# Moving the issue of a transposed activation's stores from one DMA queue to another in a fused attention and FFN kernel

## The reference

```python
x = x + xattn(layernorm(x), ctx, ctx, Wt, Wp, Wg, Wz, gn_w, gn_b)
x = x + ffn(layernorm(x), up, down, perm)

# xattn, per sample: t = Wt @ ctx, p = Wp @ layernorm(x), g = Wg @ ctx
att = sum over each of the 8 channel groups of (p * g)      # one number per group
y = Wz (block diagonal, 8 blocks of 64) @ (att * t)
out = groupnorm(y) * gn_w + gn_b + ctx

# ffn, per row of 2048: 16 heads of 128 columns picked by perm
t = gelu(t[:, perm] as (16, 128) @ up[h]) @ down[h], columns put back by the inverse of perm
```

## Time and profile before

| | before |
|---|---|
| median of three runs | 1584.0 us |
| lowest and highest | 1579.34 and 1595.7 us |
| the profiled execution | 1595.7 us, span 1593.9 us |
| mean granted TensorE clock | 0.986 |
| TensorE, VectorE, ScalarE, GpSimd busy | 95%, 75%, 67%, 61% of the span |

### The profile page before, as it was taken

How to read it: one execution, slowest core, us unless ns; L and a number is a source line. 1 busy time by engine, 2 the same in 40 slices (tenths; PEclk the granted TensorE clock), 3 DMA queues, 4 the chain that set the end, 5 groups by cost and what they waited for, 6 DMA issues and landing times.

```text
span 1593.9 us, 19526 instructions
## 1 busy us (share of the span) xinstructions
PE 1519.4 (95%) x6592; PEld 1240.8 (78%) x6592; DVE 1196.9 (75%) x1480; ACT 1066.9 (67%) x1317; POOL 977.2 (61%) x781
## 2 busy tenths in 40 slices
PE   8998879996999999999999999999999999998998
PEld 6876667875888878888788887888788887876776
DVE  5777767874788767886678876787778877878776
ACT  4634727671787738866488845878468773897876
POOL 1695646257792538917386255853579354887886
PEclk9999989998999999999999999999999999999999
DMA  8798867878476855779467783668837676759786
GB/s 319 267 317 338 247 198 276 290 219 258 138 270 240 252 163 169 265 252 260 130 195 274 255 251 122 218 251 251 251 121 264 248 233 191 252 152 258 257 280 215
DMA packets 176467, 374.79 MB, mean 235 GB/s; under 512 B 24561, under 2 KB 90097, under 8 KB 168177
## 3 DMA queue, kind: packets, MB, share of 16 engines
q1 hardware_dynamic: 151024, 281.25, 55.8%
q0 software_dynamic: 25344, 92.29, 16.5%
HBM read 287.45 MB, written 86.03 MB: 234 GB/s over the span
## 4 chain that ended last, share of the span: by engine, by line
PE 56%; DMA 11%; POOL 10%; DVE 10%; issue 6%; ACT 5%; SPq 2%; POOLq 0%; ACTq 0%; DVEq 0%
PE PP L914 16%; PE PP L899 15%; PE PP L846 12%; PE PP L860 7%; PE PP L873 5%; DMA R<-wp_scratch 4%; DVE R L1038 3%; DMA RAW<-in_cx 3%; ACT Z L987 2%; DMA WW<-w_scratch 2%; SPq L1333 2%; POOL out L1276 2%; POOL X L1261 2%; POOL FB L1268 1%; DVE FB L1173 1%
## 5 line engine op out<-in xcount | busy, mean ns | idle before, releaser
L899 PE MATMUL PP<-GG,WW 128*128 128x512 f32 x1536 | 391.2, 391 | 7.2 <-DVE GG L1178 3.8
L846 PE MATMUL PP<-R 128*128 128x512 f32 x1536 | 358.6, 393 | 15.6 <-DVE R L1038 14.5
L860 PE MATMUL PP<-R,WC 128*128 128x512 f32 x1536 | 353.4, 392 | 8.6 <-ACT Z L955 6.6
L846 PEld LDWEIGHTS PP<-R 128*128 128x128 f32 x1536 | 290.5, 190 | 79.0 <-issue 14.2
L860 PEld LDWEIGHTS PP<-R,WC 128*128 128x128 f32 x1536 | 289.7, 189 | 71.6 <-ACT Z L955 7.8
L899 PEld LDWEIGHTS PP<-GG,WW 128*128 128x128 f32 x1536 | 288.0, 188 | 71.5 <-issue 9.5
L1261 POOL TENSOR_TENSOR X<-X,RAW 128x512 f32<-128x512 f32 x128 | 203.6, 1625 | 120.4 <-DVE bn L1023 70.5
L914 PE MATMUL PP<-R,WW 128*128 128x512 f32 x1050 | 270.4, 393 | 6.4 <-DVE R L1183 3.9
L1001 ACT ACTIVATE R<-PP 128x1024 fp32r<-128x1024 f32 x175 | 179.8, 1028 | 136.3 <-PE PP L899 136.0
L1183 DVE TENSOR_TENSOR R<-PP,R 128x1024 fp32r<-128x1024 f32 x175 | 213.6, 1221 | 67.4 <-ACT PP L1002 67.4
L1002 ACT ACTIVATE PP<-PP 128x1024 f32<-128x1024 f32 x256 | 261.7, 1022 | 0.0
(11 more groups left out here) (91 smaller groups left out, 1637.0 us busy)
## 6 DMA issues: line engine op xcount, KB each, us to landing
WW<-w_scratch SPq DMA_DIRECT2D x152, 512.0 KB, 5.1
X<-in_x SPq DMA_DIRECT2D x32, 1024.0 KB, 6.3
RAW<-in_cx SPq DMA_DIRECT2D x32, 1024.0 KB, 8.9
RAW<-in_xT SPq DMA_DIRECT2D x63, 512.0 KB, 5.8
RAW<-in_cT SPq DMA_DIRECT2D x63, 512.0 KB, 7.1
xg_scratch<-FB SPq DMA_DIRECT2D x104, 256.0 KB, 4.4
w_scratch<-WW POOLq DMA_DIRECT2D x16, 1024.0 KB, 6.9
HX<-wp_scratch SPq DMA_DIRECT2D x7, 1024.0 KB, 8.1
```

The source lines that it names most:

```text
L846: t = eng.matmul(s_bank(c1), l[:, part(c1)], r, start=(dt == 0 and j == 0), stop=(dt == ND - 1 and j == 2))
L860: t = eng.matmul(PP[2 + ot // 2][:, ot % 2, :], WC[:, l, ct, part(ot)], u[:, r + ct, :], start=(ct == 0 and j == 0), stop=(ct == NT - 1 an ...
L899: t = eng.matmul(PP[slot["up", f, p]][:, e, :], wt[:, l, part(2 * p + e)], g[:, r, :], start=(j == 0), stop=(j == 2))
```

## The change

`store_x` of samples 0 to 6 is issued by GpSimd in place of SP, and is planned 0.3 units nearer to its turn. The stores of sample 7 stay on SP, and count on semaphores of their own (`xl` instead of `xg`).

```diff
     def store_x(i, q):
-        give(n.dma("xg", i, q, sem=f"xg{q}", count=4), *slot["tb", i, q])
+        give(n.dma("xg", i, q, sem=f"{'xg' if i < B - 1 else 'xl'}{q}", count=4), *slot["tb", i, q])
         order.append(("store_x", i, q))
...
-            put(t + (3 if last else 1.3), store_x, i, q)
+            put(t + (3 if last else 1), store_x, i, q)
...
     def gpsimd(eng):
...
+            elif stage == "store_x" and a[0] < B - 1:
+                i, q = a
+                pool.wait_ge(*at["tr", i, q, NT - 1])
+                for r in range(4):
+                    eng.dma_start(xg_rows(i, q, r), tb_part(i, q, r)).then_inc(S[f"xg{q}"], 16)
...
     def sync(eng):
...
-            elif stage == "store_x":
+            elif stage == "store_x" and a[0] == B - 1:
                 i, q = a
                 sp.wait_ge(*at["tr", i, q, NT - 1])
                 for r in range(4):
-                    eng.dma_start(xg_rows(i, q, r), tb_part(i, q, r)).then_inc(S[f"xg{q}"], 16)
+                    eng.dma_start(xg_rows(i, q, r), tb_part(i, q, r)).then_inc(S[f"xl{q}"], 16)
```

## The result

The kernel with the change takes 1643.0 us (median of 4 executions, 1641.5 to 1646.0) against 1585.9 us before (4 executions, on the same chip): a ratio of 1.036, interval 1.030 to 1.042. It is slower, as forecast, but by 57 us and not by 22, which is just outside the predicted range.

A forecast was written before the change was run, and what follows sets the result against it. TensorE, the busiest engine, was taken to bound the kernel, with gaps waiting for Wp. Samples 3 to 7 +30, sample 1 -10, sample 2 +2: +22 us on the median 1584.0, 1606 us, range 1576 to 1640.

The forecast's parts named there:

- the walk: Sample 3 step by step through GpSimd's stores and adds: block 3's transposes 8.4 us later, `v_mm` +5.1, +6 a sample.
- I take 4.5, because it is the same transfer: Landing of a moved store on GpSimd: 4.5 us from issue, as when SP issues it.
- The top of my bounds, 6.0 us for one landing: High end for the landing of a GpSimd store, taken from `in_down`: 6.0 us.
- adds and issue: On GpSimd: an add at 1.5 us, a DMA's issue at 0.76 us, so 3.05 us per block store.
- The rival of a dear issue: GpSimd at 0.97 us a DMA, 6.0 to land: transposes 12.4 us late, +50 in samples 3 to 7, 1634 us; chance 0.16.
- The small gap: Possible gap at y's fourth pair from block 3's column load some 4 us later; swallowed by the large gap.
- the eighth pair: Last pair of PSUM banks in y, needing ScalarE's copy: wanted at 574.1, copy done at 581.1, a 7.0 us gap.
- the clock behind the large gap: TensorE's low granted clock after the 7.0 us gap in y: 1 us more a sample than before.
- Sample 1: -10 forecast: SP's 8.45 us hold goes, Wp issued at 211 instead of 219.5, nearly all of the 9.41 us gap goes: -10 us.
- Sample 2: Sample 3's chain with four more weight loads; `v_mm` starts at 393 against 391.16: +2 us, bounds -6 and +12.
- The step to the median: Profiled execution 1595.7 us, 11.7 above the median; +22 carried to the median 1584.0 gives 1606 us.
- the cancelling rival: Block 3's transposes 4 to 6 us late, +1 to +2 in samples 3 to 7, -10 in sample 1: 1584 to 1590; chance 0.20.

The follow-up runs named there:

- all loads fenced: Changed kernel without adds in samples 3 to 7, block 3's column load held until store 0 landed, Wg, weights and Wp until store 2: 1585.0 us, 1.000.
- block 0 alone: Of the changed kernel only the stores of block 0 go to GpSimd, ahead of all adds, against the kernel before: 1600.3 us, 1.012.

## Why the prediction was right or wrong

**Right: the direction and the mechanism.** The wait for Wp vanishes in samples 2 to 7, and waits in y take its place, with ScalarE's copy behind the scaling that waits for VectorE. The wait for the transposes, put on GpSimd by itself, costs nothing (0.998). Up to store 1 the walk comes out within 0.3 us, in part by luck: store 0 went out 0.7 us later against `y_mm` than forecast, seven adds took 9.35 us and not 10.5, and the one behind them 2.46 and not 1.5. In us after the start of `y_mm` in sample 3:

| | forecast | measured | difference |
|---|---|---|---|
| store 1 starts | 18.6 | 18.9 | +0.3 |
| block 2's transposes | 25.3 | 30.6 | +5.2 |
| store 2 starts | 32.1 | 34.1 | +2.0 |
| block 3's transposes | 38.9 | 41.9 | +2.9 |
| `v_mm` starts | 51.0 | 55.3 | +4.3 |

**Wrong: "I take 4.5, because it is the same transfer".** This is the step that failed. The bytes are the same, the neighbours are not. In SP's queue the stores went out ahead of Wg and the weights; from GpSimd they are issued independently of them and fly together. Store 1 took 11.7 us from first issue to the transposes where the walk had 6.8. Separating them shows it. From first issue to the next transposes, over samples 3 to 7, block 1's store takes 11.0 to 12.0 us after the change, 7.3 to 7.6 with Wg and weights later, and 7.0 to 8.1 with all loads fenced; block 2's takes 7.8 to 9.3, 10.0 to 10.7 and 7.0 to 7.2. So block 3's transposes came 11.7 us late in the mean of the five samples, where the walk had 8.4. The top of my bounds, 6.0 us for one landing, was also too low; it came from a row whose own maximum was 10.4.

**Over-priced: adds and issue.** The two groups of seven adds ran at 9.35/7 = 1.34 and 8.77/7 = 1.25 us each where I took 1.5, DMAs at 0.65 where I took 0.76. So store 2 did not wait for adds but, for 3.78 us, for VectorE. This hid part of the first error: +5.2 shrank to +2.0. The rival of a dear issue gave 1634, the nearest of my numbers, but half for the wrong reason: the issue was cheap, only the landing was long.

**The small gap: another cause, but swallowed, as forecast.** I looked for it in the fourth block's column load. It comes from block 2's transposes: ScalarE's copy waits for them (7.20 us at 565.04, it reuses Z), and `y_lo` runs behind them. It adds nothing to the time: whatever the first gap was, the eighth pair starts 6.34 to 6.36 us behind block 3's transposes in all five samples, and the walk had 6.3. Without the first gap the second would only be longer. Whether the first makes the clock behind the second worse, no run shows.

**Mis-sized as well: the clock behind the large gap.** The walk ran the eighth pair in 5.5 us and priced the clock at 1 us a sample. The pair took 7.29 us in sample 3 and 7.2 to 8.6 in the five, 2.3 more in the mean than at the even rate; `v_mm` behind it then ran without a slow stretch, in 12.4 us where it had taken 12.5 to 14.1. So from block 3's transposes to `v_mm` it took 13.5 us, where I had 12.1.

**Sample 1: -10 forecast, -2.8 measured.** Wp went out at 213.25 against the forecast 211, and the matmul came at 224.04, 10.8 us later, where I took 8.4: Wg went out 0.4 us ahead of it. Again a transfer's time was taken without its company. That brought `v_mm` forward by 5.4 us against `y_mm`. Another 2.6 were lost inside it, at a place where the walk had put nothing: the first gathers wait for block 3's store, which stands behind adds and weight work on GpSimd and goes out at 217.36 in place of 211.05. GpSimd's first gather and TensorE's gap for it, inside `v_mm` (the gather went out at 225.73 before):

```profile
231.25 1.07 POOL L1254 DMA_INDIRECT FB<-xg_scratch,perm_sb  x1 [6.92 <-DMA xg_scratch<-SMM]
```

```profile
237.46 1.62 PE L899 MATMUL PP<-GG,WW 128*128 128x512 f32 x6 [2.37 <-DVE GG L1178]
```

Sample 2 was +0.9 against +2.

**The sizes, summed.** Samples 3 to 7 lost 48.2 us against 30, sample 1 gave back 7 us less than forecast, sample 2 was 1 better: 46 in place of 22 in these parts. Some 3 us came back outside these parts, so the traced executions differ by 43. The step to the median, which I took as equal for both, added the other 14. It isn't all chance: the profiled execution of before was probably slow in just the waits that the change removes. The kernel with the wait alone, equal in time, was profiled in an execution 9.7 us shorter, and 8 of these lie between `y_mm` and the end of `v_mm` in samples 1 to 7 (in sample 2 it spends 52.8 us from y to v, the profiled one of before 56.6). The sum of the cancelling rival is off by some 3 us, and nothing rests on it: five times +1 to +2, -10 and the +2 of sample 2 make 1581 to 1586, not 1584 to 1590.

**How the 57 us divide.** Without adds the move costs 18 us (1604.9 against 1586.7), and with the loads fenced it ends at 1585.0, net of the gain at Wp. The other 39 come with the adds' place. But these aren't two fixed shares. With adds, holding back loads alone gave back 26 us, and from there leaving out the adds gave only 4 more (1614.5 to 1610.4), since the stores then meet Wg. A store's place among the adds also decides which loads it meets.

**Open.** A fenced store of block 2 takes 7.2 us on GpSimd; SP's took 7.7 in sample 3 before (558.68 to 566.36), with two weight loads ahead of it. Whether GpSimd's path has a share of its own, of some tenths of a us, isn't settled. Nor do the runs tell whether the stores landed early on SP because its queue kept the loads behind them, or only because the loads were issued some 4 us later (Wg at 551.79, 3.8 us behind store 1's first issue, against 0.15 after). Why block 0 alone raises the wait for Wp to 38.0 us wasn't followed further.

## What to carry to other kernels

A DMA queue also spaces its transfers out: taking small urgent stores out of it lets the big loads behind them be issued at the same moment and fly beside them, so price a moved DMA by its landing in the new company, and look at what is issued within some microseconds of it. Move only those for which the new engine is idle (here block 3's, a quarter of the change, -17 us in place of +57), and try first whether the one late load can simply be issued earlier. When a walk along a chain gives a lateness, follow everything that hangs on each late step, such as the gathers here, and give the matmuls behind a gap the slow clock in the walk itself.

## What the runs showed of the hardware

The same 112 stores of 256 KB are 528 packets each on SP's queue ((151024 - 91888) / 112) and 80 each on GpSimd's ((34304 - 25344) / 112). Their issue on GpSimd takes a steady 0.65 us each, the longest 0.795, even with VectorE busy beside it (block 2's four in sample 3, 567.16 to 569.74, run beside `y_lo`), while SP's four took from 3.1 to 8.45 us. So fewer packets and a cheaper issue went with a slower kernel. The section "Who interferes with whom" of the Trainium skill's "SBUF — State Buffer", by which VectorE could hold up a DMA that GpSimd issues, isn't borne out in size here: 0.14 us at most over the median.

An instruction of VectorE can be held for many microseconds while GpSimd works on other data. VectorE's `sum_c` of 128x4 takes 0.16 to 0.17 us in samples 3 to 7 of the kernels without adds. Where it started inside a group of GpSimd's adds, it could last until one of them ended, most often the last: 12.00 us in the kernel with the adds of block 1 behind store 1, and 6.08 in sample 1 of the kernel before, from 195.77 to 201.85, where the adds end at 201.82. In all 17 cases of over 1.5 us in the kept traces, it ends 0.02 to 0.03 us behind an add. It isn't so each time: in sample 3 of the kernel before it took 0.32 us in the middle of nine adds. VectorE's rows of the kernel before, samples 1 and 3:

```profile
195.77 6.08 DVE L1054 SCALAR_TENSOR_TENSOR scol<-mv,scol 128x4 f32<-128x4 f32 x1
...
555.34 0.32 DVE L1054 SCALAR_TENSOR_TENSOR scol<-mv,scol 128x4 f32<-128x4 f32 x1
```

What decides was not tested.
